# Moving the time-mix gating and the skip sum of batches 2 and 3 from VectorE to GpSimd

## The reference

```
for i in 0, 1:                          # time-mix layers
    n = layer_norm(x) * w + b
    k, v, r = n Wk^T, n Wv^T, sigmoid(n Wr^T)
    state_t = 0.95 * state_(t-1) + 0.05 * k_t * v_t
    x = x + (r * state) Wo^T
h = layernorm(x_in + x)                 # the skip sum
logits = h Wrouter + b; top 2 of 8 experts, softmax of the two
o_e = silu((h_e Wfc + b) * (h_e Wgate + b)) Wproj + b   # 307 slots per expert and batch
out = layernorm(h + sum of probability * o_e over the two experts)
```

## Time and profile before

| what | us |
|---|---|
| median of 3 runs (lowest to highest) | 401.93 (401.17 to 403.64) |
| the profiled execution, its own time | 401.28 |
| its span in the trace | 399.5 |
| PE busy in the span | 323.6 |
| DVE busy | 268.3 |
| POOL busy | 208.3 |
| ACT busy | 159.7 |

### The profile page before, as it was taken

One profiled execution on the slowest core, in us unless ns is written; L12 is line 12 of the kernel. 1 busy time (PEld: TensorE's weight loads), 2 busy tenths in 40 slices (PEclk: granted clock), 3 DMA queues, 4 the chain that ended last, 5 costly groups with the idle time before them and its releaser, 6 DMA issues.

```text
span 399.5 us, 6793 instructions
## 1 busy us (share of the span) xinstructions
PE 323.6 (81%) x2171; PEld 273.0 (68%) x2171; DVE 268.3 (67%) x846; ACT 159.7 (40%) x292; POOL 208.3 (52%) x245
## 2 busy tenths in 40 slices
PE   6876866777999999999999999998899888895000
PEld 3433454245988979998897998897798887894000
DVE  6698967387866878968687787782456675752134
ACT  2525411112654453555544454342554544451000
POOL 4446844875035463334556648456466558300674
PEclk9998756888999999999999999899999999999555
DMA  7763184114013113311111432132163132121112
GB/s 225 222 58 105 53 256 128 39 42 136 2 37 88 36 52 103 85 38 38 47 49 46 121 88 73 29 92 79 46 173 82 40 99 71 51 58 32 39 53 66
DMA packets 53058, 31.73 MB, mean 79 GB/s; under 512 B 12704, under 2 KB 48807, under 8 KB 53024
## 3 DMA queue, kind: packets, MB, share of 16 engines
q1 hardware_dynamic: 47840, 22.99, 20.9%
q0 software_dynamic: 4096, 8.06, 7.2%
q10 hardware_dynamic: 1088, 0.26, 0.3%
HBM read 18.92 MB, written 12.71 MB: 79 GB/s over the span
## 4 chain that ended last, share of the span: by engine, by line
PE 54%; DVE 14%; issue 11%; POOL 10%; DMA 4%; ACT 3%; another core or an unknown queue 2%; POOLq 0%; SPq 0%; DVEq 0%; ACTq 0%
PE ps_o L622 16%; POOL picked L1114 4%; POOL slot_rows L1084 3%; PE pair0g L608 2%; PE bank L489 2%; PE pair0g L610 2%; PE pair1g L608 2%; DVE prod L998 2%; PE bank L499 2%; PE bank L497 2%; PE bank L469 2%; PE pair0g L609 2%; PE pair0h L610 2%; PE pair0h L608 2%
## 5 line engine op out<-in xcount | busy, mean ns | idle before, releaser
L622 PE MATMUL ps_o<-proj_sb,hidden 128*104 128x128 f32 x768 | 97.7, 275 | 4.1 <-DVE o_sb L1007 2.1
L1084 POOL DMA_INDIRECT slot_rows<-x_ln,row_to x64 | 71.2, 1112 | 48.1 <-DVE prod L998 27.0
L622 PEld LDWEIGHTS ps_o<-proj_sb,hidden 128*104 128x104 f32 x768 | 90.9, 171 | 6.2 <-issue 3.1
L1114 POOL DMA_INDIRECT picked<-expert_rows,row_from x64 | 66.4, 1037 | 54.0 <-issue 19.3
L735 ACT ACTIVATE gate_s<-pair0g,bgate_sb 128x308 f32<-128x308 f32 x64 | 33.0, 516 | 83.6 <-PE pair0g L610 71.8
L998 DVE SCALAR_TENSOR_TENSOR prod<-pair1h,bfc_sb,gate_s 128x308 f32<-128x308 f32 x64 | 33.9, 530 | 27.2 <-ACT gate_s L735 16.0
L998 DVE SCALAR_TENSOR_TENSOR prod<-pair0h,bfc_sb,gate_s 128x308 f32<-128x308 f32 x64 | 34.0, 531 | 24.7 <-ACT gate_s L735 18.5
L742 ACT ACTIVATE hidden<-prod 128x616 f32<-128x616 f32 x64 | 45.5, 711 | 9.5 <-DVE prod L998 7.7
L735 ACT ACTIVATE gate_s<-pair1g,bgate_sb 128x308 f32<-128x308 f32 x64 | 32.9, 515 | 26.4 <-PE pair1g L610 23.0
L608 PE MATMUL pair1g<-slotT_hi,gate_hi 128*128 128x308 f32 x64 | 26.5, 414 | 6.2 <-DVE prod L998 4.2
L608 PE MATMUL pair0g<-slotT_hi,gate_hi 128*128 128x308 f32 x64 | 25.9, 404 | 3.9 <-DVE prod L998 2.9
(11 more groups left out here) (148 smaller groups left out, 722.7 us busy)
## 6 DMA issues: line engine op xcount, KB each, us to landing
slot_x<-slot_rows SPq DMA_DIRECT2D x20, 256.0 KB, 3.4
expert_rows<-o_sb SPq DMA_DIRECT2D x32, 156.0 KB
x_in<-in_L_attn_h SPq DMA_DIRECT2D x4, 512.0 KB, 5.4
prod<-in_L_ffn_w_gate SPq DMA_DIRECT2D x8, 256.0 KB, 2.7
prod<-in_L_ffn_w_c_fc SPq DMA_DIRECT2D x8, 256.0 KB, 3.1
proj_sb<-in_L_ffn_w_c_proj SPq DMA_DIRECT2D x8, 256.0 KB, 5.9
out<-picked SPq DMA_DIRECT2D x16, 128.0 KB, 2.1
slot_rows<-slot_x SPq DMA_DIRECT2D x5, 256.0 KB, 4.5
```

The source lines that it names most:

```text
L622: mm = nc.tensor.matmul(ps_o[0:PART, P * part:P * part + P], hidden[:, e % 2, c, PART * part:PART * part + PART], proj_sb[:, e, c, :], sta ...
L1084: nc.gpsimd.indirect_dma_start(out=slot_rows, out_offset=bass.IndirectOffsetOnAxis(ap=row_to[:, c:c + 1], axis=0), in_=x_ln[:, b % RING, c ...
L1114: nc.gpsimd.indirect_dma_start(out=picked[:, j, k, :], out_offset=None, in_=expert_rows[b % 2], in_offset=bass.IndirectOffsetOnAxis(ap=row ...
```

## The change

For b = 2 and 3 VectorE's `mix` ends with the scan. GpSimd does the gating in two instructions (add 1 in place, then multiply by the state), and the skip sum in one; for batches 0 and 1, in the head, all stays on VectorE. In GpSimd's queue a stage of `POOL_MIX` stands after the scatter of the same point.

```
-              16: [("norm", 2)], 17: [("add", 1)], 18: [("stats", 3)], 19: [("norm", 3)], 20: [("skip_sum", 0)],
-              21: [("mix", 2)], 23: [("mix", 3)], 24: [("add", 2)], 25: [("stats", 4)], 27: [("add", 3)],
+              16: [("norm", 2)], 17: [("add", 1)], 18: [("stats", 3)], 19: [("norm", 3)], 21: [("mix", 2)], 23: [("mix", 3)], 24: [("add", 2)], 25: [("stats", 4)], 27: [("add", 3)],
...
-POOL_MIX = {15: [("rstd", 2)], 17: [("rstd", 3)], 26: [("rstd", 4)], 31: [("rstd", 5)]}
+POOL_MIX = {11: [("gate", 0)], 14: [("gate", 1)], 15: [("rstd", 2)], 17: [("rstd", 3)], 20: [("skip_sum", 0)],
+            21: [("gate", 2)], 23: [("gate", 3)], 26: [("rstd", 4)], 31: [("rstd", 5)]}
...
+                if b < 2:
+                    dve.wait_ge(r_copied, c)
+                    dve.wait_ge(state_made, c)
+                    nc.vector.scalar_tensor_tensor(mixed[:, lo:hi], mixed[:, lo:hi], 1.0, kv_sb[:, lo:hi],
+                                                   ALU.add, ALU.mult).then_inc(mixed_made, 1)
...
+            def gate_of(b, n):
+
+                lo, hi = HALF * (n % 2), HALF * (n % 2) + HALF
+                pool.wait_ge(r_copied, step(b, n))
+                nc.gpsimd.tensor_scalar(mixed[:, lo:hi], mixed[:, lo:hi], 1.0, None, ALU.add).then_inc(r_shifted, 1)
+                pool.wait_ge(r_shifted, step(b, n) - 8)
+                pool.wait_ge(state_made, step(b, n))
+                nc.gpsimd.tensor_tensor(mixed[:, lo:hi], mixed[:, lo:hi], kv_sb[:, lo:hi], ALU.mult)\
+                  .then_inc(mixed_made, 1)
+
+            def skip_sum(b, _):
+
+                pool.wait_ge(x_added, step(b, 1))
+                pool.wait_ge(normed_made[0], step(b, 1))
+                nc.gpsimd.tensor_tensor(x_in[:, b % 2, :, :], x_in[:, b % 2, :, :], x_mid[:, b % 2, :, :], ALU.add)\
+                  .then_inc(skip_made, 1)
```

More of the change, by code:

```diff
@@ L299, in time_mix_moe @@
         state_made = sem("state_made")
+        r_shifted = sem("r_shifted")
         mixed_made = sem("mixed_made")
@@ L848, in mix @@
                   .then_inc(state_made, 1)
-                dve.wait_ge(r_copied, c)
-                dve.wait_ge(state_made, c)
-                nc.vector.scalar_tensor_tensor(mixed[:, lo:hi], mixed[:, lo:hi], 1.0, kv_sb[:, lo:hi],
-                                               ALU.add, ALU.mult).then_inc(mixed_made, 1)
+                if b < 2:
[3 more added lines that the diff above has]
+                                                   ALU.add, ALU.mult).then_inc(mixed_made, 1)
             def add(b, n):
@@ L1099, in low @@
                                         ALU.subtract).then_inc(weights_split, 1)
-            stages = {"low": low, "rstd": rstd_of, "shares": shares, "scatter": scatter_tile}
+            stages = {"low": low, "rstd": rstd_of, "gate": gate_of, "skip_sum": skip_sum, "shares": shares, "scatter": scatter_tile}
             def gather(b, c):
```

## The result

The changed kernel takes 407.89 us in the median of 4 runs (407.8 to 413.56), the kernel before 402.64 in 4 runs beside it (401.17 to 403.64). The ratio is 1.0161, with a 95% interval of 1.011 to 1.0212: slower by 1.6%, some 6.5 us by the ratio and 5.25 by the medians. Three of the four runs lie within 0.1 us of one another; the fourth, 413.56, lifts the ratio. The profiled execution took 407.89 us against 401.28, 6.6 more.

What follows compares the result with a forecast made beforehand. TensorE, busy 29.9 of 30 us, was taken to bound the kernel; lateness of GpSimd's queue reaching it costs 2.0 + 2.5 = 4.5 us, so 401.93 + 4.5 = 406.4 us, range 401.6 to 409.5.

Steps and rivals of the forecast that it cites:

- TensorE is full, VectorE's relief is worth nothing: Periods 0 and 1: 8.0 us leave VectorE, nothing gained; at most 0.3 us of TensorE's idle time in a period returns.
- The durations on GpSimd: Moved instructions: multiply 1.27 us, add 0.65, skip sum 2.4; 10.4 us of GpSimd's queue per period.
- The add of 1: First instruction of each gating on GpSimd: taken as 0.65 us, bounded by 0.52 (memset) and 1.27 (two-input form).
- The path of points 20 to 24: GpSimd's back-to-back queue in period 0: last scatter ends at 157.45 instead of 152.54, slots' load 4.9 us later.
- Whoever comes first holds the other: VectorE's scans against GpSimd's instructions and scatters: the later one is held; scan of n = 2 ends at 148.0, not 146.1.
- `out` of n = 3 waits 1.0 us: TensorE, period 0: gating 3 ends at 156.3, `out` was to start at 155.35; a 1.0 us wait.
- The slots: Load before TensorE's first slot transpose at point 28: first group late, 1.6 to 2.5 us total delay in period 0.
- The sum: Total over both periods: 2.0 us in period 0 plus 2.5 in period 1, 4.5 us.
- The margins: Rival at `out` and the slots: scatters not stretched, 0 to 0.6 us a period, 401.6 to 403.1 us; chance 0.15.
- The scan did not get in first: Rival at point 20: scan precedes and holds the sum, 2.4 to 3.3 us a period, 407 to 408.5; chance 0.12.
- The clock: Rival: TensorE's clock falls after one or two new pauses, 1.8 us each, 408 to 410 us; chance 0.18.
- ScalarE's wait: Rival: ScalarE's 5.20 us wait at 279.9, or the clock's fall, goes or shortens: 398 to 404.6 us; chance 0.10.

Runs made afterwards that it cites:

- GpSimd's idle stretches alone: Kernel before, with only the gatings of n = 0 and 1 and the skip sum (at point 17) moved to GpSimd: 393.22 us, ratio 0.9997.

## Why the prediction was right, and where not

The forecast was 406.4 us, and 407.89 came, which is 0.4 above the span that it gave its likeliest case (404.9 to 407.5). The mechanism is the one it named: an added 5.9 us between the first and the last product for the 4.5 of the sum. That the number lies so near is in part luck, since terms that were off had opposite signs. Its steps:

- *TensorE is full, VectorE's relief is worth nothing.* Right: with GpSimd's idle stretches alone the relief moves nothing. What I missed is how small the relief is: VectorE's busy time fell by 3.7 us, not 8; of the difference 3.0 us are the two held scans (2.62 and 2.87 for 1.23).
- *The durations on GpSimd.* The multiply (1.26 to 1.28 for 1.27) and the sum (2.38 for 2.4) were right, the sum with a fixed part that no row had shown. **The add of 1 is the mis-sized term**: 0.65 forecast, 1.50 to 1.52 on the path, beyond my upper bound of 1.27. The failing step is the ground for choosing: the memset and the select, near in what they touch, are other instructions than this one, and the two-input form, which I took for an upper bound, is none. The Trainium skill (GPSIMD Engine Reference, 3.1 Elementwise) gives 769 ns over 512 elements, measured, as the best case of a tight loop, and sets it against the price of two inputs. The trace doesn't bear that out for this form, which takes 1499 ns. By that figure the sum would have been about 5.0 us, short of the 5.9 as well.
- *The path of points 20 to 24.* The two adds made it 1.7 us longer than forecast, and yet the last scatter's record ended at 157.75, only 0.3 after the 157.45 of the forecast, once I take off the 0.28 us by which the period started later. On the same count scatter 11 ended 0.4 us earlier than forecast, and scatter 12 ended 1.90 us after the sum and not 2.05; scatter 13, which I had stretched as in the earlier trace rows, began 0.06 us after its scan and not 0.14 and took 1.08 us, which gave back 0.8. Right for partly wrong reasons: with the right add I would have had this path 1.4 us too long.
- *Whoever comes first holds the other.* Right for the scan behind the sum, in both kernels with the sum at point 20 (2.62 and 2.87, 2.90 and 2.91), though I had put the sign at over 3 us. With the gatings alone the other order shows too: the adds of 1 that GpSimd began while a scan ran took 1.92 and 1.78 us in period 0 for 1.50, and ended 1.3 us after the scan. The scan's hold costs nothing by itself, as the skip sum alone shows. The Trainium skill (SBUF — State Buffer, Who interferes with whom) expects this hold; it infers none by a two-input VectorE instruction on the making of DMA descriptors; the scatter of 1.73 us begun at 146.73 beside the scan, where others take 0.97, agrees with my reading of the earlier trace rows and not with that inference. The scatter of 1.08 us, begun 0.06 us after its scan, shows that it isn't regular.
- *`out` of n = 3 waits 1.0 us.* 1.11 and 1.10. `out` of n = 2 keeps its margin; points 11 and 14 cost nothing, as said.
- *The slots.* Load at 158.7 forecast, 160.29 measured. 1.0 us of it is the last scatter, whose landing took 2.26 us for the 1.25 that I had carried over from the earlier trace rows. `rstd` behind it is excluded; in all ten late landings an instruction transfer lies beside it, in period 1 of the changed kernel none does (232.62 to 233.87, 1.25 us); whether it is the cause stays open. The rest is the path's 0.3. This is what makes period 0 3.1 us instead of 2.0. The group's own landing, 2.8 us in period 0 and 3.2 in period 1, lay within 2.6 to 3.5.
- *The sum.* 3.1 + 2.7 for 2.0 + 2.5; the 0.3 and 0.4 at the two ends are no term of mine, and a difference of this size between two executions says nothing.
- *The rivals.* The margins did not hold; but each half of the change alone shows that they hold for half of it, so this rival was near. Its point of decision, put at 2.4 to 3.3 us of lateness, was 1.8 to 2.2, the late landing being the difference. The scan did not get in first. The clock did not fall in the periods of the changed kernel; in the experiments it fell after pauses of 2.35 us and more. The length of the pause alone does not decide it: in the kernel before it fell after the pause of 0.85 us at 248 and stayed at 1.00 over one of 2.26 us that ended at 281.20. ScalarE's wait stayed.

How much hung on that one duration, by an estimate: without any add the last scatter is 2.4 us late, two adds of 0.65 would make it 3.7, and less the 2.0 or so of margin that is 1.7 us in a period, some 3 in all, 0.8% and within what a measurement tells from no change. No version measured here is faster than the kernel before beyond its interval.

## What to carry to other kernels

Moving work off an engine that doesn't bound the kernel wins nothing by itself; what it costs is read at the receiving engine, from what stands behind the new instructions in its queue, above all DMAs whose landing a full engine waits for. Such costs are no sum: two edits that cost nothing measurable alone can use up one margin together, and the same sum three points earlier, in an idle stretch of the queue, takes most of the loss back (1.0026 for 1.0146). Price each moved instruction by the same form on the receiving engine, and measure it alone if the trace has no such row.

## What the runs showed of the hardware

- On GpSimd an add of a constant over 128x512 takes 1.50 us as a tensor-scalar instruction with one operation and 0.62 with two; half the width takes 0.86, the two-input form 1.26, the two-input form with a broadcast column 1.04, a copy 0.61.
- TensorE's granted clock was 0.50 to 0.59 in a window after each pause of 2.35 to 5.3 us (two kernels, both periods); after pauses of 1.1 and 1.7 us with 4.6 us of work between them it stayed at 1.00. In period 2 of the kernel before it fell to 0.50 after a pause of 0.85 us and stayed at 1.00 after one of 2.26.
- A sigmoid between silus costs two table loads of 1.28 us each; tanh there costs none.
- An instruction of GpSimd or VectorE that begins while a long one of the other runs can be held: a scan of 1.23 us took 2.62 to 2.91 beside GpSimd's sum, an add of 1.50 took 1.92 beside a scan, a scatter's issue of 0.97 took 1.73 to 1.94.
- The last scatter's landing freed the load 1.24 to 1.29 us after the end of its record in 18 of 28 places and 1.64 to 2.62 us after it in ten. All ten, and only one of the 18, had a transfer of an instruction queue within 0.3 us before and 0.7 after that end.
